# First loads and constant fills split and moved, masked keys in four steps on GpSimd, and a new order of all steps, in a two-layer transformer kernel

## The chip, the cores and the metric

One core of a Trainium2 chip. A time is the device time in microseconds of one execution; each version is given by the median of its runs. "The span" is the part of the profiled execution that the profiler's records cover. TensorE has two clock levels, 1.2 and 2.4 GHz; a granted clock of 0.5 in a row is the lower one, 1.0 the upper.

## The reference

Two layers are applied to x (16 sequences of 128 tokens, 128 features), each conditioned on a vector per sequence and on a context of 120 tokens. All in fp32. Cut to what matters:

```python
# layer 0 (c = cond, context = ctx), 16 heads of 8
shift_a, scale_a, gate_a, shift_m, scale_m, gate_m = split(silu(c) @ W_mod + b_mod, 6)
q, k, v = split(modulate(_ln(x), shift_a, scale_a) @ W_qkv + b_qkv, 3)
x = x + gate_a * (softmax(q k^T * scale) v @ W_proj + b_proj)
x = x + (cross attention of _ln(x) @ W_qc with _ln(context) @ W_kvc) @ W_cproj + b_cproj
x = x + gate_m * (gelu_tanh(modulate(_ln(x), shift_m, scale_m) @ W_mlp1 + b_mlp1) @ W_mlp2 + b_mlp2)
# layer 1: three adaptive norms (gamma, beta from c @ ln_w.T + ln_b), rope on q and k
x = x + attn(rope(q), rope(k), v) @ sa_out_w.T          # from adaln1(x) @ qkv_w.T
x = x + attn(rope(q), rope(k of context), v of context) @ ca_out_w.T
x = x + gelu_erf(adaln3(x) @ ffn_w1.T + ffn_b1) @ ffn_w2.T + ffn_b2
```

The modulation therefore consists of twelve vectors per sequence (six of layer 0, six of layer 1), each a product of a 128x128 weight block with the condition, plus a bias. The first self-attention needs only the first two of them, shift_a and scale_a.

## The kernel before

The 16 sequences are worked on in four **streams** of four sequences (CB = 4, so 512 tokens at a time). There are four attentions (a = 0: self, layer 0; 1: cross, layer 0; 2: self, layer 1; 3: cross, layer 1), so 16 **units** f = 4a + s, and eight MLPs m (four for each layer). x stays in SBUF throughout.

A unit goes through these steps. `stats` (VectorE, bn_stats and bn_aggr, L578 and L581) is followed by rstd on GpSimd (L744, L747); `ln` normalises (VectorE, xn, L588); `xT` transposes on TensorE (L873) and ScalarE applies the modulation while it copies (xnT, L829). `k`, `q`, `v` are the projections (L911, L918). In layer 1 rope follows on VectorE (L603, L608). `khi`/`qhi` round to the high part (ScalarE, Kh and Qh, L803 and L806), `klo`/`qlo` give the rest (VectorE, Kl and Ql, L617 and L620). `kstore`/`qstore` write these to DRAM, `kload`/`qload` read them back in the layout of the scores (Ks, Qd). `kmask` (GpSimd, Kd, L763) makes four copies of the keys, each with only the rows of some heads. `max` (TensorE L929, VectorE L683) finds the maximum of each row of scores, in four blocks b of four products each; `mT`, `mstore`, `mload` bring the maxima into a row of Qd. Then eight `score` steps (TensorE L949, exponential on ScalarE L843) and eight `value` steps (TensorE L966), `copy`, `norm`, `aT` and the output projection (`o` and `yT`, or `out`), which ends in an update of x (VectorE L727). An MLP has `stats`, `ln`, `xT`, four `h` (TensorE L992, GELU on ScalarE L860), and `h2` with `yT` (layer 0; L998) or `out` (layer 1; L1012).

The order of all this is written out by a table T of times (in steps, 16 to a unit), with one entry for each attention or layer: `make_plan` gives every step of every unit a time, sorts, and each engine issues its steps in that order, one after another. TensorE, GpSimd and the DMA queue of SyncE go by `plan`; VectorE and ScalarE go by `late`, the same list sorted by a second time, which differs only for `h`. An engine waits, by semaphores, where a step's input isn't there yet, and everything behind that step waits too. Five PSUM banks (ps_misc) are used in turn, in the order of `plan`.

Before the loop come the loads and the preparation. SyncE's queue issues x of stream 0, the 776 KB of modulation weights with the condition (`first`, which shares the tile hT), 512 KB of layer-0 weights, x of the other streams, the context twice, the other weights (1792 KB). ScalarE's queue issues the biases and the constants (identity, cos, sin). `small_in` counts three loads: `first`, biases, constants. GpSimd fills V (0, and 1 in the columns that sum), and, after the first rstd, Ks (1) and the two halves of Qd (0). VectorE makes `head_rows`, a sum over the identity, and inside the first `stats` the SiLU of the condition (`condition`, L627 to L631); TensorE then runs all twelve modulation products (L882), and VectorE adds the biases after the first `ln` (`modulation`, L639). ScalarE's first `xT` waits for all twelve.

## Time and profile before

| | us |
|---|---|
| median of 3 runs | 483.98 (481.41 to 486.79) |
| the profiled execution | 484.73 |
| its span | 482.9 |
| TensorE busy | 391.4 (81% of the span), mean granted clock 0.90 |
| VectorE busy | 330.1 (68%) |
| ScalarE busy | 267.9 (55%) |
| GpSimd busy | 159.0 (33%) |

An engine's busy share is a mean over the whole span: the stretches of the kernel have different limits, so the table is to be read with the rows by stretch below. Matmuls are pipelined and their ends are modelled, so TensorE's share says the least. An fp32 matmul shows up as two records.

### The profile page before, as it was taken

Reading aid. Unit: us, or ns where it says so; the run is one execution under the profiler, and the core shown is the slowest. Engines: PE = TensorE matmul, PEld = TensorE weight load, DVE = VectorE, ACT = ScalarE, POOL = GpSimd, SP = SyncE. Lnnn points to the kernel's source line nnn. Section 1 sums busy time; section 2 is a strip of 40 time slices with the busy share of each in tenths; the row PEclk is TensorE's granted clock in tenths of the full one; section 3 lists DMA queues with packets and bytes.
Section 4 is the critical chain, followed back from the end, with each engine's and each line's share of the span. In section 5 each row is a group of like instructions: output and inputs, shape, how many; then the busy total and the mean of one; then the engine's idle time right before and its main releaser. Section 6 shows DMA issues by size and latency. Waiting matters only on the chain.

```text
span 482.9 us, 9958 instructions
## 1 busy us (share of the span) xinstructions
PE 391.4 (81%) x3744; PEld 240.0 (50%) x3744; DVE 330.1 (68%) x841; ACT 267.9 (55%) x503; POOL 159.0 (33%) x138
## 2 busy tenths in 40 slices
PE   1555889888889797797987887989889898979686
PEld 1422455556555544434534534556565554737464
DVE  2656768999999837728648736799999884721331
ACT  1112457667676664565475554576576665666552
POOL 4764263455283401701601601335154161020130
PEclk9965599999999997978899958799999897979989
DMA  8860837558584516124225213346657551420001
GB/s 251 288 196 0 237 87 213 162 177 231 142 213 141 131 69 126 48 90 106 71 92 101 76 71 90 84 150 167 155 156 191 150 141 69 114 42 23 3 1 44
DMA packets 31271, 59.20 MB, mean 123 GB/s; under 512 B 3455, under 2 KB 7807, under 8 KB 30975
## 3 DMA queue, kind: packets, MB, share of 16 engines
q1 hardware_dynamic: 30935, 58.35, 43.9%
q8 instruction: 30, 0.49, 0.4%
q10 hardware_dynamic: 288, 0.21, 0.2%
q14 instruction: 18, 0.15, 0.1%
HBM read 31.81 MB, written 26.74 MB: 121 GB/s over the span
## 4 chain that ended last, share of the span: by engine, by line
PE 47%; DVE 21%; ACT 11%; POOL 9%; issue 5%; DMA 4%; SPq 2%; ACTq 0%; DVEq 0%; POOLq 0%
DVE maxima L683 8%; PE ps_misc L992 8%; PE ps_ao L966 8%; PE ps_misc L911 7%; POOL Kd L763 6%; PE ps_sc L949 6%; DVE xn L588 5%; PE ps_misc L1012 5%; ACT PT L843 5%; PE ps_misc L873 4%; ACT xnT L829 4%; PE ps_misc L998 3%; PE ps_misc L929 2%; POOL rstd L747 2%; DVE stats L578 2%
## 5 line engine op out<-in xcount | busy, mean ns | idle before, releaser
L843 ACT ACTIVATE PT<-ps_sc 128x512 f32<-128x512 f32 (+1 forms) x256 | 138.9, 596 | 79.8 <-PE ps_sc L949 79.0
L683 DVE TENSOR_REDUCE maxima<-ps_misc 128x4 f32<-128x512 f32 (+1 forms) x256 | 154.1, 666 | 29.4 <-PE ps_misc L929 29.1
L763 POOL TENSOR_SCALAR Kd<-Kh,head_rows 128x512 fp32r<-128x512 f32 (+1 forms) x64 | 98.6, 1556 | 114.2 <-ACT Kh L803 87.4
L949 PE MATMUL ps_sc<-Qd,Ks 57*128 57x256 f32 (+1 forms) x512 | 65.7, 335 | 18.6 <-ACT PT L843 15.6
L966 PE MATMUL ps_ao<-PT,V 120*18 120x128 f32 (+1 forms) x2048 | 71.6, 279 | 2.8 <-ACT PT L843 2.7
L744 POOL TENSOR_SCALAR vareps<-mv 128x4 f32<-128x4 f32 (+1 forms) x28 | 6.8, 242 | 188.5 <-DVE mv L581 188.0
L949 PEld LDWEIGHTS ps_sc<-Qd,Ks 57*128 57x128 f32 (+1 forms) x512 | 38.6, 187 | 55.7 <-ACT PT L843 28.4
L966 PEld LDWEIGHTS ps_ao<-PT,V 120*18 120x18 f32 (+1 forms) x2048 | 50.7, 99 | 20.9 <-issue 9.6
L829 ACT ACTIVATE xnT<-ps_misc,vec 128x128 f32<-128x128 f32 x80 | 30.1, 458 | 45.5 <-PE ps_misc L873 33.7
L911 PE MATMUL ps_misc<-xnT,W 128*128 128x512 f32 x72 | 47.5, 784 | 5.1 <-ACT xnT L829 5.1
L929 PE MATMUL ps_misc<-Kd,Qh 32*128 32x512 f32 (+1 forms) x256 | 45.3, 535 | 7.6 <-POOL Kd L763 6.5
L588 DVE TENSOR_SCALAR xn<-x,mv,rstd 128x128 f32<-128x128 f32 x96 | 36.6, 519 | 11.1 <-POOL rstd L747 11.1
L992 PE MATMUL ps_misc<-xnT,W 128*128 128x512 f32 x64 | 41.2, 803 | 3.7 <-ACT xnT L829 3.7
L727 DVE TENSOR_TENSOR x<-ps_misc,x 128x512 f32<-128x512 f32 x24 | 16.5, 688 | 38.1 <-PE ps_misc L1012 34.8
L873 PE MATMUL ps_misc<-cst,xn 128*128 128x128 f32 x96 | 18.5, 325 | 24.4 <-DVE xn L588 22.3
L929 PEld LDWEIGHTS ps_misc<-Kd,Qh 32*128 32x128 f32 x256 | 18.9, 197 | 26.2 <-issue 8.0
L860 ACT ACTIVATE hT<-ps_misc,bias 128x512 f32<-128x512 f32 x32 | 22.0, 687 | 16.7 <-PE ps_misc L992 16.4
L747 POOL TENSOR_TENSOR rstd<-vareps,minus_half 128x4 f32<-128x4 f32 (+1 forms) x28 | 29.3, 1047 | 2.3
L714 DVE TENSOR_SCALAR yT_sb<-ps_misc,bias,vec 128x128 f32<-128x128 f32 x32 | 10.9, 403 | 24.8 <-PE ps_misc L998 24.8
L992 PEld LDWEIGHTS ps_misc<-xnT,W 128*128 128x128 f32 x64 | 15.9, 262 | 23.8 <-issue 17.9
L873 PEld LDWEIGHTS ps_misc<-cst,xn 128*128 128x128 f32 x96 | 12.2, 163 | 29.8 <-issue 23.6
L911 PEld LDWEIGHTS ps_misc<-xnT,W 128*128 128x128 f32 x72 | 15.9, 246 | 19.6 <-issue 10.1
(75 smaller groups left out, 455.2 us busy)
## 6 DMA issues: line engine op xcount, KB each, us to landing
Qd<-q_mem SPq DMA_DIRECT2D x64, 192.0 KB
k_mem<-Kh SPq DMA_DIRECT2D x16, 512.0 KB, 3.2
q_mem<-Qh SPq DMA_DIRECT2D x16, 512.0 KB, 3.4
Ks<-k_mem SPq DMA_DIRECT2D x32, 192.0 KB
Ks<-k_mem SPq DMA_DIRECT2D x32, 180.0 KB
k_mem<-Kl SPq DMA_DIRECT2D x16, 256.0 KB, 3.6
q_mem<-Ql SPq DMA_DIRECT2D x16, 256.0 KB, 2.9
W<-weights SPq DMA_DIRECT2D x1, 1792.0 KB, 18.9
```

The lines of the kernel that those rows point to most:

```text
L588: dve.tensor_scalar(dst[0:rows, b, :], src[0:rows, b, :], mv[0:rows, which, b, 0:1], rstd[0:rows, which, b:b + 1], ALU.subtract, ALU.mult) ...
L683: dve.tensor_reduce(maxima[:, HG * n:HG * n + HG, st.b], bank(st.use + n)[:, 0:HG * ns].rearrange("p (h k) -> p h k", h=HG), AX_X, ALU.max ...
L747: pool.tensor_tensor(rstd[0:rows, which, :], vareps[0:rows, which, :], minus_half[0:rows, :], ALU.pow).then_inc(S["rstd_ready"], 1)
L763: pool.tensor_scalar(Kd[:, st.f % 2, c, 0:n], f32(Kh[:, st.f % 2, 0:n]), head_rows[:, c:c + 1], None, ALU.mult).then_inc(S["kd_ready"], 1)
L829: act.activation(dst[:, b * P:(b + 1) * P], src[:, b * P:(b + 1) * P], ACT.Identity, scale=vec[:, c, m:m + 1], bias=vec[:, c, sh:sh + 1]). ...
L843: act.activation(PT[0:ns, st.k % PSLOTS, g, :, :, :].rearrange("p i e t -> p (i e t)"), ps_sc[0:ns, g, :], ACT.Exp, scale=SCALE).then_inc( ...
L873: last = pe.transpose(bank(use)[:, b * rows:(b + 1) * rows], src[0:rows, b, :], ident[0:rows, 0:rows])
L911: pe.matmul(bank(st.use + i)[:, 0:n], w(f"{st.kind}{st.a}{form}"), src[:, 0:n], start=True, stop=True).then_inc(S["misc_filled"], 1)
L929: pe.matmul(bank(st.use + n)[:, 0:HG * ns], Qh[rows, st.f % 2, st.b * P:(st.b + 1) * P], Kd[rows, st.f % 2, :, st.b * ns:(st.b + 1) * ns], ...
L949: ins = pe.matmul(ps_sc[0:ns, side, i * E * P:(i + 1) * E * P], Ks[rows, st.f % 2, n, st.b * ns:(st.b + 1) * ns], Qd[rows, st.f % 2, n, :, ...
L966: last = pe.matmul(ps_ao[32 * c:32 * c + PAIR, st.b * P:(st.b + 1) * P], heads[:, at:at + PAIR], PT[0:ns, st.k % PSLOTS, c // E, odd, c % ...
L992: pe.matmul(bank(st.use), w(f"w1_{st.a}", st.j), xnT[:, feeds["mlp", st.m] % 2, :], start=True, stop=True).then_inc(S["misc_filled"], 1)
```

## The change

Four things are edited.

1. **Loads.** The condition (64 bytes a row) is loaded first, on its own, and only it counts for `small_in`. Then come x of stream 0, the first two of the twelve modulation blocks (128 KB, `mod_in0`), the layer-0 weights, x of stream 1, the other ten blocks (640 KB, `mod_in1`), and the rest as before.
2. **Modulation in two parts.** Two products stand ahead of the loop, with their two bias additions after the first `ln`. The other ten are a step of their own, `mods`, placed right behind the first `q` on TensorE and on VectorE. ScalarE's first `xT` waits for two vectors; the ones with another modulation wait for all.
3. **Fills.** VectorE fills the first half of Qd at the start; GpSimd fills Ks at the start, V only after the first `ln` (it waits for xn), and the second half of Qd behind the masked keys of unit 0. `head_rows` moves behind the first two bias additions, and VectorE's wait for the three small loads goes.
4. **Order.** `kmask` becomes four steps, spaced by kstep, so that others can fall between them, and many entries of T change.

```diff
@@ the table T (entries that change) @@
-    hstep=(0.0, 0.08),
+    hstep=(0.0, 0.01),
-    ln=(-36.9, -31.68, -33.31, -37.7),
-    xT=(-32.06, -29.2, -31.0, -33.04),
-    k=(-30.42, -33.11, -28.7, -30.27),
-    q=(-27.8, -25.66, -28.55, -28.51),
-    v=(-26.93, -32.58, -25.07, -25.11),
+    ln=(-36.9, -31.68, -33.31, -37.8),
+    xT=(-32.14, -29.39, -31.19, -33.23),
+    k=(-30.42, -32.7, -28.7, -30.22),
+    q=(-27.81, -25.66, -28.45, -28.51),
+    v=(-26.65, -32.58, -24.18, -25.26),
+    kstep=(0.3, 0.3, 0.3, 0.3),
-    max=(-23.26, -22.48, -23.15, -22.04),
-    mstep=(1.04, 0.96, 1.04, 0.85),
-    mT=(-9.62, -8.09, -7.7, -8.99),
+    max=(-23.26, -22.39, -23.06, -21.95),
+    mstep=(1.02, 1.02, 1.04, 0.85),
+    mT=(-9.62, -8.09, -8.17, -8.99),
-    copy=(1.29, -0.71, 0.74, 0.13),
-    norm=(2.85, 0.41, 2.69, 2.61),
+    copy=(1.29, -0.24, 0.74, 0.13),
+    norm=(2.69, 0.41, 2.69, 2.61),
...
-    yT=(10.12, 10.03, 6.38, 10.59),
+    yT=(9.35, 9.26, 5.61, 9.8),
-    mh=(9.79, 12.57),
-    mh2=(11.4, 15.76),
-    myT=(12.58, 13.02),
+    mh=(10.22, 13.1),
+    mh2=(11.43, 15.76),
+    myT=(11.93, 12.79),
...
-    qlo=(0.75, 1.08, 3.94, 3.39),
+    qlo=(0.75, 1.08, 5.75, 3.39),
-    value=(4.0, 3.57, 4.26, 5.04),
-    cln=(-39.87, -39.68, -41.82, -39.07),
+    value=(4.04, 3.61, 4.3, 5.07),
+    cln=(-40.26, -39.98, -42.12, -38.02),
...
@@ make_plan @@
-        at(t + T["kmask"][a], Step("kmask", **who))
+        for c in range(HG):
+            at(t + T["kmask"][a] + c * T["kstep"][a], Step("kmask", h=c, **who))
...
+    rest = Step("mods")
+    rest.late = [st for st in plan if st.kind == "q" and st.f == 0][0].late
+    plan.insert([st.kind for st in plan].index("q") + 1, rest)
@@ SyncE: loads @@
+                at, width = WCOLS["condT"]
+                sp.dma_start(first[:, at:at + width], weights[:, at:at + width]).then_inc(S["small_in"], 16)
                 load_x(0)
-                sp.dma_start(first, weights[:, 0:W_FIRST]).then_inc(S["small_in"], 16)
+                sp.dma_start(first[:, 0:MODS * D], weights[:, 0:MODS * D]).then_inc(S["mod_in0"], 16)
                 sp.dma_start(W[:, 0:W_SECOND - W_FIRST], weights[:, W_FIRST:W_SECOND]).then_inc(S["weights_in"], 16)
-                for s in range(1, STREAMS):
+                load_x(1)
+                sp.dma_start(first[:, MODS * D:at], weights[:, MODS * D:at]).then_inc(S["mod_in1"], 16)
+                for s in range(2, STREAMS):
                     load_x(s)
@@ VectorE @@
-                def modulation():
+                def modulation(part):
-                    dve.wait_ge(S["mod_products"], 1)
-                    for v in range(NV):
+                    dve.wait_ge(S["mod_products"], part + 1)
+                    for v in (range(MODS), range(MODS, NV))[part]:
...
                 dve.memset(ps_ao[:, :], 0.0).then_inc(S["sums_zeroed"], 1)
-                dve.wait_ge(S["small_in"], 48)
-                dve.tensor_reduce(head_rows[:, :], ident.rearrange("p (n c d) -> p c n d", n=NG, c=HG), AX_XY,
-                                  ALU.add).then_inc(S["rows_ready"], 1)
+                dve.memset(f32(Qd[:, 0, :, :, :]), 0.0).then_inc(S["zeros_ready"], 1)
...
                         if st.k == 0:
-                            modulation()
+                            modulation(0)
+                            dve.tensor_reduce(head_rows[:, :], ident.rearrange("p (n c d) -> p c n d", n=NG, c=HG),
+                                              AX_XY, ALU.add).then_inc(S["rows_ready"], 1)
+                    elif st.kind == "mods":
+                        modulation(1)
@@ GpSimd @@
                 fill(0, minus_half[:, :], -0.5)
-                fill(1, V[:, :, :, :, :], 0.0)
-                fill(2, V[:, :, :, :, HD:VW], 1.0)
+                fill(1, f32(Ks[:, :, :, :]), 1.0)
...
                         if st.norm_no == 0:
-                            fill(3, f32(Ks[:, :, :, :]), 1.0)
-                            for half in range(2):
-                                fill(4 + half, f32(Qd[:, half, :, :, :]), 0.0)
+                            pool.wait_ge(S["xn_ready"], CB)
+                            fill(2, V[:, :, :, :, :], 0.0)
+                            fill(3, V[:, :, :, :, HD:VW], 1.0)
                     elif st.kind == "kmask":
...
+                        if st.f == 0 and st.h == HG - 1:
+                            fill(4, f32(Qd[:, 1, :, :, :]), 0.0)
@@ ScalarE, xT @@
                         if st.k == 0:
+                            act.wait_ge(S["vec_ready"], MODS)
+                        elif st.spec["mult"] not in (None, MULT_A):
                             act.wait_ge(S["vec_ready"], NV)
@@ TensorE @@
+                def modulate(part):
+                    pe.wait_ge(S[f"mod_in{part}"], 16)
+                    for v in (range(MODS), range(MODS, NV))[part]:
+                        lhs, rhs = ((w_first("mod", v), silu[:, 2, :]) if v < 6 else
+                                    (w_first("ln", v - 6), condT))
+                        last = pe.matmul(ps_sc[:, part, v * B:(v + 1) * B], lhs, rhs, start=True, stop=True)
+                    last.then_inc(S["mod_products"], 1)
                 pe.wait_ge(S["silu_done"], 1)
-                for v in range(NV):
...
+                modulate(0)
...
+                    elif st.kind == "mods":
+                        modulate(1)
```

What the new times do to the order on each engine, unit by unit: the last block of `max` of unit 0 goes before `k` of unit 1 on TensorE, and the third block of `max` of unit 1 before `xT` of unit 2; in streams of the first attention a `score` step goes before the two `value` steps that stood ahead of it; in the MLPs of layer 0 the sixth `score` step goes before the four `h`, and `yT` before the seventh; in those of layer 1 two `value` steps or an `out` swap places with their neighbour; `qlo` of layer 1's self-attention moves behind the first block of `max`.

## Rows read from the trace of the kernel before

**Rows 1.** The page: busy us, share of the span and instructions of each engine.
```profile
PE 391.4 (81%) x3744; PEld 240.0 (50%) x3744; DVE 330.1 (68%) x841; ACT 267.9 (55%) x503; POOL 159.0 (33%) x138
```

**Rows 2.** Stretches: length, PE, PEld, DVE, ACT, POOL busy; clock, DMA share, GB/s.
```profile
117.00:136.00 19.00, 16.83 (x219) 11.18 (x215) 18.67 (x54) 13.19 (x26) 9.79 (x10) 1.00 0.64 173
...
180.00:320.00 140.00, 115.95 (x944) 65.27 (x944) 92.45 (x231) 75.44 (x139) 36.60 (x33) 0.84 0.33 87
```

**Rows 3.** Timeline, first 26 us: start us, busy us, engine, line, tiles, idle before.
```profile
8.41 0.86 DVE L578 BATCH_NORM_STATS2 stats<-x 128x6 f32<-128x128 f32 x4
...
10.09 1.05 POOL L747 TENSOR_TENSOR rstd<-vareps,minus_half 128x4 f32<-128x4 f32 x1
...
11.10 3.50 POOL L735 MEMSET Ks<- 128x4096 f32 x1
...
11.18 7.17 DVE L588 TENSOR_SCALAR xn<-x,mv,rstd 128x128 f32<-128x128 f32 x4 [0.94 <-POOL rstd L747]
...
14.66 7.13 POOL L735 MEMSET Qd<- 128x4096 f32 x2
...
18.27 1.79 DVE L639 TENSOR_SCALAR vec<-ps_sc,bias 128x16 f32<-128x16 f32 x12
...
18.40 1.11 PE L873 MATMUL ps_misc<-cst,xn 128*128 128x128 f32 x4 [2.81 <-DVE xn L588]
...
20.16 1.50 ACT L829 ACTIVATE xnT<-ps_misc,vec 128x128 f32<-128x128 f32 x4 [11.73 <-DVE vec L639]
...
21.71 3.52 PE L911 MATMUL ps_misc<-xnT,W 128*128 128x512 f32 x4 [2.19 <-ACT xnT L829]
```

**Rows 4.** Timeline, 0 to 37 us: fill of PSUM, modulation products, first masked keys, maxima.
```profile
0.91 0.48 DVE L643 MEMSET ps_ao<- 128x512 f32 x1 [0.91 <-PEq L1083]
...
12.88 2.72 PE L882 MATMUL ps_sc<-hT 128*128 128x16 f32 x12
...
24.61 6.20 POOL L763 TENSOR_SCALAR Kd<-Kh,head_rows 128x512 fp32r<-128x512 f32 x4 [2.81 <-ACT Kh L806]
...
31.69 4.88 DVE L683 TENSOR_REDUCE maxima<-ps_misc 128x4 f32<-128x512 f32 x8 [3.75 <-PE ps_misc L929]
...
36.48 1.11 DVE L588 TENSOR_SCALAR xn<-x,mv,rstd 128x128 f32<-128x128 f32 x4
```

**Rows 5.** DMA issues before 30 us: count, KB each, us from issue to landing.
```profile
x<-x_in SPq DMA_DIRECT2D x1, 256.0 KB, 4.6
...
cst<-consts ACTq DMA_DIRECT2D x1, 192.0 KB, 7.0
...
W<-weights SPq DMA_DIRECT2D x1, 512.0 KB, 7.7
...
W<-weights SPq DMA_DIRECT2D x1, 1792.0 KB, 18.9
```

**Rows 6.** Timeline of the ramp, 43 to 70 us.
```profile
43.25 1.89 DVE L683 TENSOR_REDUCE maxima<-ps_misc 128x4 f32<-128x512 f32 x3 [2.08 <-PE ps_misc L929]
...
61.28 0.69 ACT L806 ACTIVATE Kh<-ps_misc,bias 128x512 fp32r<-128x512 f32 x1 [1.28 <-PE ps_misc L911]
...
63.32 6.20 POOL L763 TENSOR_SCALAR Kd<-Kh,head_rows 128x512 fp32r<-128x512 f32 x4
```

**Rows 7.** Timeline of two MLPs of the first layer.
```profile
169.51 1.28 ACT L860 ACT_TABLE_LOAD   x1
...
169.59 3.67 PE L992 MATMUL ps_misc<-xnT,W 128*128 128x512 f32 x8 [0.62 <-ACT xnT L829]
...
170.80 1.47 ACT L860 ACTIVATE hT<-ps_misc,bias 128x512 f32<-128x512 f32 x2
...
174.13 3.67 PE L998 MATMUL ps_misc<-hT,W 128*128 128x512 f32 x8 [0.44 <-ACT hT L860]
...
206.44 6.72 PE L992 MATMUL ps_misc<-xnT,W 128*128 128x512 f32 x8 [0.48 <-ACT xnT L829]
```

**Rows 8.** One microsecond from the table of stretches, columns as in rows 2.
```profile
28.00:29.00 1.00, 0.00 (x0) 0.00 (x0) 0.00 (x0) 0.00 (x0) 1.00 (x1) 0.63 1.04 385
```

54 lines of the change are left out of this document (27 added, 27 removed).

## The prediction

> **What bounds the kernel now.** I read the page first for the shares. VectorE is busy for 68% of the span, TensorE for 81% [rows 1]: neither fills it, so the question is where each one is the limit, and the table of stretches answers it. From about 98 to 155 us VectorE is the limit: the stretch shown, a third of that, has it busy for 18.67 of 19 us [rows 2]. In such a stretch an order that only helps TensorE or ScalarE brings nothing. From 180 to 320 us no engine is full (VectorE 92 of 140 us, TensorE 116 at a mean granted clock of 0.84): a serial chain sets the time there, from the update of x over norm, transpose, keys, masked keys and the MLP to the next update [rows 2]. The timeline of the first 45 us shows that the whole pipeline starts late: the first key product runs at 21.71 us [rows 3] and the first maxima at 31.69 us [rows 4]. All queues run in order and wait for each other, not for a time of day. So what the first stage loses is lost at the end, and what it wins arrives there, unless something later eats it.
>
> **Why the start is late.** The four normalisations of the first stream (xn) should cost about 1.1 us, as the same four do for the second stream at 36.48 us [rows 4]. They take 7.17 us, from 11.18 to 18.35 [rows 3]. GpSimd fills Ks from 11.10 and the two halves of Qd from 14.66 on, at 3.5 us a fill, and VectorE gets through only once the second of these three fills has ended, at about 18.2 us. The Trainium skill (SBUF — State Buffer, § Who interferes with whom) says that VectorE's tensor_scalar in a two-port mode and GpSimd share a port pair that is held for a whole instruction, and the trace agrees (7.17 against 1.11 us). Then come twelve small bias additions, 1.79 us, all of which the first xnT waits for (20.16) [rows 3].
>
> **Part 1: loads and fills, up to the first key product.** After the change stream 0 waits for its own load alone. That load landed 4.6 us after its issue at 0.72, at 5.3 us [rows 5]; behind the small condT load it is issued some 0.45 us later, so 5.8. VectorE first fills Qd's first half: no VectorE fill of SBUF is in the trace; 512 elements of PSUM took 0.485 us [rows 4], so 4096 take 3.9, and I take 4, from 1.4 to 5.4 us. The low bound is half of that, the high one a wait for GpSimd's Ks fill (now from 0.9 to 4.4 us), which would end it at 8.4. So statistics 5.8 to 7.0, rstd at 8.3 (0.2 and 1.05 us and the hops between) [rows 3]. But the step `condition` stands before xn in VectorE's queue and waits for the constants, which landed 7.0 us after 1.16, at 8.2 [rows 5]; the bytes in flight around them are hardly fewer, so I keep 8.2 (bound: 7.3, where rstd decides). The exponential and the three small steps end at 9.1. xn is then 9.1 to 10.2, since GpSimd now waits for xn before it fills V. Only two of twelve products stand before the transposes, 0.9 us by the rate of [rows 4] (12 records, six products, in 2.72 us: some 0.44 us a product), and two additions, 0.3 us. The transposes took 1.1 us and the xnT 1.5 us [rows 3]: 10.3 to 11.4, 11.5 to 13.0. **First key product at 13.1 instead of 21.7 us: 8.6 us gained.** Its weights landed 7.7 us after 1.62, at 9.3 [rows 5], with more ahead of them than now.
>
> The Trainium skill (SBUF — State Buffer, § Who interferes with whom) says that a VectorE instruction outside the two-port modes with at most one SBUF input does not contend with GpSimd, and VectorE: DVE Perf Modes (§ Zero memsets can be issued as uint32) that a memset takes a cycle per element; no run here shows either yet. By these the fill ends near 5.7 us and the sum stays; were the port shared after all, the sum would be 2.4 us worse, 479.4.
>
> **Part 2: what the other ten products cost.** They now stand behind the first q. On TensorE that is 10 x 0.44 = 4.4 us, from 3.5 us after the key product to 7.9, and v (1.0 us) follows: 9.0. The masked keys are done 2.9 + 6.2 = 9.1 us after the key product, as before (24.61 and 6.20 against 21.71) [rows 4], so TensorE's part is hidden under GpSimd's. VectorE's is not quite: it sits in order behind these products until 7.9, then adds ten biases (1.5), computes Ql (0.75) and the statistics of stream 1 (1.25): free for the first maxima at 11.55, where it was at 9.98 (31.69 - 21.71). **1.6 us lost.** Ql's store comes later with it, at about 23.5 us, but its reader, the first score, is some 25 us away. The load of these ten weights is issued fifth; about 1.8 MB lie before its end, and the load of 512 KB had landed at 9.3 with as much asked for. Lower bound for its landing 9, upper bound 24.2, where the last large load landed [rows 5]; needed at 16.6.
>
> **Part 3: fills behind the first masked keys.** V's fill, smaller than those of 3.5 us, takes GpSimd from 10.2 to at most 13.7, under a wait for Kh until 16. The fill of Qd's second half, 3.5 us, now stands before the rstd of stream 1, which would be ready 14 us after the key product; its reader, xn of stream 1, comes after eight maxima (5.3 us), at 16.9. Hidden; without that cover it would cost up to 3.5.
>
> **Part 4: masked keys as four steps.** Sorting both tables of times, only one of GpSimd's neighbours changes: the statistics of stream 0's context (cstats) fall between the second and third quarter of the masked keys of unit 3. It brings one rstd forward by two quarters (3.1 us) and delays two quarters by 1.3 us, in the stretch where VectorE is the limit. I take zero. In the serial stretch the norm before each MLP still stands behind all four quarters (6.2 us), so the split doesn't shorten that chain.
>
> **Part 5: order in the ramp, 38 to 70 us.** The last maxima products of unit 0 now go before the next key product. VectorE had waited 2.08 us for them [rows 6]. Most of that is cut off by unit 1's masked keys, which start no earlier for it. Statistics of stream 3 come earlier, so GpSimd no longer makes unit 2's masked keys wait for their rstd: they started at 63.32 though Kh had been there since 61.97 [rows 6]. **I take this 1.3 us as gained** (0 to 2.1).
>
> **Part 6: order in the serial stretch.** In the four MLPs of the first layer one pair of exponentials (1.08 us) moves from behind the four GELUs to before them, between xnT and the table load of 1.28 us [rows 7]. TensorE's first product isn't ready before the load ends, so load and exponentials no longer fit under it: for the first MLP, exponentials to 170.6, load to 171.9, four GELUs of 0.7 to 174.7. The second product, which waits for all four and began at 174.13, starts at 174.85, 0.7 us later, and with it the update of x. Where the clock is low the GELUs are paced by TensorE (6.72 instead of 3.67 us for the first product) [rows 7] and nothing is lost. Two MLPs are of each kind: **1.4 us lost** (0 to 2.8). The Trainium skill (ScalarE: Activation LUTs, § What ACT_TABLE_LOAD costs) adds a drain of 1.38 us to each switch; here hT starts 0.01 us after the load's end, so the trace speaks against it and I give it no chance; by the page the sum would be 2.8 us worse, 479.8. Elsewhere scores now go before a pair of values in streams 0 to 3, but mostly where VectorE is the limit: zero. In the second layer and at the tail such swaps change at most 1 us in either direction: zero.
>
> **The sum.** -8.6 + 1.6 - 1.3 + 1.4 = -6.9 us. The profiled execution took 484.73 us (span 482.9), so 477.8; the median of the three runs is 483.98, 0.75 below, so I forecast 477.0. Its own range is 472 to 481 (bounds of parts 1, 5 and 6, and the clock). About 1% is what a measurement of this kernel can tell from no change.
>
> **Rivals.** (A) *The lead is gone before the first maxima.* The ten products hold VectorE's queue: if TensorE's clock is low there, as it is from the 29th microsecond on now [rows 8], they take 8.8 instead of 4.4 us, and the time is 481.4; if their weights land only with the last large load, at 24.2, the first maxima come at 32 and nothing is left of the lead: 484. For it: the clock falls in a microsecond in which TensorE had nothing to do [rows 8]. Against: the DMA order puts these weights fifth, and TensorE has work at 10, 11 and 13 us. (B) *Given back later.* The GELU delay hits all four MLPs, with a missed slot in the chain (masked keys before rstd, 6.2 us) once: -8.6 + 1.6 + 2.8 + 1.3 gives 481. For it: that chain has no slack. Against: GpSimd's order there is unchanged. (C) *The clock turns against it: slower.* Of the eight MLPs, four run their first products at the low clock, as the one at 206.44, and four at the high one, as the one at 169.59 [rows 7]. Place: the products behind xnT, where the moved pair of scores and values shifts TensorE's work. Price 3.05 us each [rows 7]. From three of four on, the 7 us are gone; with all four it is 489.2, slower by 1.1%. Against: the relative order around them is nearly the same. (D) *More than summed*: the clock turns the other way for two or more (6.1 us, 470.9), or xn is held back less by masked keys. (E) *The start isn't shortened*, because xn is stretched anyway: 484. Against: no fill is left that could run beside it, so I fold it into (A).
>
> **How the numbers follow.** Forecast as summed 0.60, (A) with (E) 0.19, (B) 0.10, (C) 0.05, (D) 0.06. Faster by over 1% (below 479.1): forecast and (D), 0.66. Within 1%: (A) and (B), 0.29. Slower: (C), 0.05. The range reaches down into (D) and up over most of (A) and (B): 472 to 482.5; about 0.05 lies below and 0.12 above.
>
> **What would show it.** xn of stream 0 at 1.1 us; the first key product at 12.3 to 13.5 us; the ten later products ending about 8 us after it and the first maxima 11.5 us after it; the first score 7 to 9 us earlier; VectorE's full stretch of the same length; first GELU 1.1 us later after xnT in the MLPs at the high clock; the number of MLPs with slow first products still four. I'd be wrong if the constants land later than 8.2 us, if the ten weights land after 17, or if the distance from the first score to the end grows by over 3 us.

## The result: 2% slower, not 1.4% faster

| | before | after |
|---|---|---|
| median, us | 483.09 (481.41 to 486.79, 4 runs) | 493.62 (492.53 to 496.31, 4 runs) |
| ratio after / before | | 1.0192, 95% interval 1.0144 to 1.0240 |
| profiled execution, us (span) | 484.73 (482.9) | 492.53 (490.7) |
| first key product, us | 21.71 | 12.75 |
| first maxima on VectorE, us | 31.69 | 22.44 |

Ratios, here and below, leave out single executions that ran slower than the others of their kernel, so a ratio can differ from the quotient of the two medians.

The forecast was 477.0 us with a range of 472 to 482.5. The kernel lies 11 us above that range. The head start is there, and in this execution larger than forecast (9.25 us at the first maxima, forecast 7.0); the rest of the kernel takes some 17 us more.

The page of the profile after, busy us, share and instructions of each engine (as [rows 1]):

```profile
PE 396.4 (81%) x3744; PEld 244.2 (50%) x3744; DVE 327.1 (67%) x842; ACT 266.2 (54%) x503; POOL 155.1 (32%) x137
```

The work is nearly the same. TensorE's busy time grew by 5.0 us at the same number of instructions (mean granted clock 0.89 after, 0.90 before); that of the other three engines fell by 2 to 4 us. So for VectorE, ScalarE and GpSimd the 8 us more of span are idle time. Where? First the timeline of the first 26 us after (start us, busy us, engine, line, operation, tiles, number; in brackets the engine's idle time before it and who ended it), which answers to [rows 3, 4]:

```profile
0.88 3.51 POOL L748 MEMSET Ks<- 128x4096 f32 x1
...
2.23 3.47 DVE L655 MEMSET Qd<- 128x4096 f32 x1 [0.84 <-issue]
...
6.26 0.21 ACT L794 ACTIVATE silu<-hT 128x16 f32<-128x16 f32 x1 [3.34 <-DMA cst<-consts]
...
8.87 1.12 DVE L599 TENSOR_SCALAR xn<-x,mv,rstd 128x128 f32<-128x128 f32 x4 [0.94 <-POOL rstd L759]
...
11.20 1.50 ACT L845 ACTIVATE xnT<-ps_misc,vec 128x128 f32<-128x128 f32 x4 [4.72 <-PE ps_misc L889]
...
12.75 3.50 PE L932 MATMUL ps_misc<-xnT,W 128*128 128x512 f32 x4 [1.59 <-ACT xnT L845]
...
15.65 6.20 POOL L775 TENSOR_SCALAR Kd<-Kh,head_rows 128x512 fp32r<-128x512 f32 x4 [2.12 <-ACT Kh L820]
...
16.90 1.49 PE L900 MATMUL ps_sc<-hT 128*128 128x16 f32 x12
...
18.43 1.52 DVE L650 TENSOR_SCALAR vec<-ps_sc,bias 128x16 f32<-128x16 f32 x10 [2.09 <-PE ps_sc L900]
...
22.44 3.68 DVE L696 TENSOR_REDUCE maxima<-ps_misc 128x4 f32<-128x512 f32 x6 [0.65 <-PE ps_misc L952]
```

xn is 1.12 us and no longer 7.17, the key product starts 8.96 us earlier and the first maxima 9.25 us earlier. Up to here nothing went wrong.

A marker follows the lead further: ScalarE copies the turned maxima (maxT) exactly once in each of the 16 units (a unit is one attention of one stream; attention 0 has units 0 to 3, attention 1 has 4 to 7). Its start, before and after, in us:

| unit | 0 | 1 | 2 | 3 | 4 | 5 | 6 | 7 | 9 | 11 | 13 | 15 |
|---|---|---|---|---|---|---|---|---|---|---|---|---|
| before | 46.91 | 66.84 | 86.98 | 106.61 | 126.01 | 145.85 | 166.64 | 200.94 | 275.84 | 336.35 | 374.48 | 421.46 |
| after | 34.87 | 58.98 | 80.03 | 101.70 | 126.49 | 150.13 | 172.89 | 211.54 | 288.33 | 344.80 | 384.51 | 428.70 |
| after - before | -12.0 | -7.9 | -7.0 | -4.9 | +0.5 | +4.3 | +6.3 | +10.6 | +12.5 | +8.5 | +10.0 | +7.2 |

The lead of 12 us (7.9 with the new start alone, e16) is down to 7 at unit 2, is gone by unit 4, and 6 us more are lost by unit 6. The 13 us between units 2 and 6 are lost where VectorE had been full: before, from about 98 to 155 us, of which [rows 2] shows a part. The table of stretches after, 80 to 160 us (length, then PE, PEld, DVE, ACT, POOL busy; granted clock, DMA share, GB/s):

```profile
80.00:100.00 20.00, 17.49 (x213) 11.59 (x214) 17.00 (x51) 12.52 (x25) 9.26 (x9) 0.91 0.60 162
100.00:120.00 20.00, 15.02 (x166) 9.79 (x164) 15.08 (x40) 10.52 (x21) 5.00 (x5) 0.87 0.71 202
120.00:140.00 20.00, 17.62 (x209) 10.92 (x207) 17.32 (x52) 11.88 (x23) 7.85 (x9) 0.93 0.51 136
140.00:160.00 20.00, 18.35 (x207) 11.79 (x203) 16.46 (x50) 10.60 (x20) 7.77 (x8) 0.86 0.41 121
```

VectorE is no longer full there: it is busy 65.9 of 80 us. Before, it was busy 76.7 us of the same stretch. And TensorE's granted clock, 1.00 in each of these four rows before, is now 0.86 to 0.93. The engine that set the pace waits; the next rows show for what. Timeline after, around the worst place (unit 5's keys and values):

```profile
109.52 1.12 PE L939 MATMUL ps_misc<-W,cnT 128*120 128x128 f32 x8
...
111.06 1.11 DVE L599 TENSOR_SCALAR xn<-x,mv,rstd 128x128 f32<-128x128 f32 x4
...
113.39 0.50 PE L974 MATMUL ps_sc<-Qd,Ks 57*128 57x256 f32 x4 [2.75 <-DMA Qd<-m_mem]
...
113.83 1.07 PE L991 MATMUL ps_ao<-PT,V 128*18 128x128 f32 x32
115.02 0.61 ACT L830 ACTIVATE V<-ps_misc 120x512 f32<-120x512 f32 x1 [5.16 <-PE ps_ao L991]
115.52 0.65 ACT L820 ACTIVATE Kh<-ps_misc,bias 128x480 fp32r<-128x480 f32 x1
...
116.20 0.72 DVE L631 SCALAR_TENSOR_TENSOR Kl<-ps_misc,bias,Kh 128x480 fp32r<-128x480 f32 x1 [4.04 <-ACT Kh L820]
116.27 2.96 POOL L775 TENSOR_SCALAR Kd<-Kh,head_rows 128x480 fp32r<-128x480 f32 x2 [5.91 <-ACT Kh L820]
```

Read it from the bottom. GpSimd stands 5.91 us and VectorE 4.04 us for Kh. Kh stands behind ScalarE's copy of V, which waited 5.16 us. V has three buffers (VSLOTS = 3), so unit 5's copy waits for the last value product of unit 2, at 113.83. That product now stands behind the first score of unit 3 (113.39), which waited 2.75 us for its load of the maxima. Three order changes meet in this chain: Kh behind V (ScalarE), values behind the next score (TensorE), and a late load (SyncE). SyncE's own queue, after, shows why the load is late:

```profile
101.98 0.50 SPq L556 DMA_DIRECT2D m_mem<-maxT  x1
102.52 1.15 SPq L523 DMA_DIRECT2D k_mem<-Kh  x1
```

Unit 4's Kh has been there since 91.8 us, but its store stands behind the store of unit 3's maxima, which waits for those maxima (engine and line, who is waited for: us in total, times, longest):

```profile
SPq L556 <- ACT maxT L852: 10.6, 1, 10.6
```

So the stores and then the loads of Qd, which follow in the same queue, all go out in one bunch from 102 to 109 us.

### The profile page after: what moved, and what is told of

The parts are those of the page before. It is cut to its first block, busy times and chain, and to the rows that moved or that the text cites. A ratio compares the mean times of both kernels' runs of the same rounds, so it can differ in the third digit from the quotient of the medians.

```text
span 490.7 us, 9979 instructions
## 1 busy us (share of the span) xinstructions
PE 396.4 (81%) x3744; PEld 244.2 (50%) x3744; DVE 327.1 (67%) x842; ACT 266.2 (54%) x503; POOL 155.1 (32%) x137
## 4 chain that ended last, share of the span: by engine, by line
PE 50%; ACT 18%; DVE 13%; issue 6%; POOL 6%; DMA 4%; SPq 3%; ACTq 0%; DVEq 0%; POOLq 0%
PE ps_sc L974 8%; PE ps_ao L991 8%; PE ps_misc L932 8%; ACT PT L859 7%; PE ps_misc L1037 5%; POOL Kd L775 5%; DVE maxima L696 5%; PE ps_misc L952 5%; PE ps_misc L889 4%; PE ps_misc L1023 3%; ACT hT L876 3%; PE ps_misc L1017 3%; PE ps_misc L1000 3%; ACT xnT L845 3%; PE ps_misc L939 2%
## 5 line engine op out<-in xcount | busy, mean ns | idle before, releaser
L974 PE MATMUL ps_sc<-Qd,Ks 57*128 57x256 f32 (+1 forms) x512 | 68.9, 349 | 25.3 <-ACT PT L859 20.4
L991 PE MATMUL ps_ao<-PT,V 120*18 120x128 f32 (+1 forms) x2048 | 75.9, 290 | 3.4 <-ACT PT L859 3.4
L952 PE MATMUL ps_misc<-Kd,Qh 32*128 32x512 f32 (+1 forms) x256 | 50.1, 542 | 13.7 <-POOL Kd L775 6.7
L932 PE MATMUL ps_misc<-xnT,W 128*128 128x512 f32 x72 | 46.5, 770 | 2.7 <-ACT xnT L845 2.5
L952 PEld LDWEIGHTS ps_misc<-Kd,Qh 32*128 32x128 f32 x256 | 21.1, 200 | 35.6 <-issue 9.6
L599 DVE TENSOR_SCALAR xn<-x,mv,rstd 128x128 f32<-128x128 f32 x96 | 28.7, 361 | 10.1 <-POOL rstd L759 10.1
L1017 PE MATMUL ps_misc<-xnT,W 128*128 128x512 f32 x64 | 31.8, 643 | 3.5 <-ACT xnT L845 3.5
L704 DVE RECIPROCAL rden<-ps_misc 128x32 f32<-128x32 f32 x32 | 11.3, 354 | 26.8 <-PE ps_misc L1000 26.6
L1000 PE MATMUL ps_misc<-cst,AOs 128*128 128x128 f32 x128 | 23.6, 314 | 6.1 <-ACT AOs L865 5.0
L727 DVE TENSOR_SCALAR yT_sb<-ps_misc,bias,vec 128x128 f32<-128x128 f32 x32 | 10.9, 404 | 22.8 <-PE ps_misc L1023 22.0
L830 ACT ACTIVATE V<-ps_misc 128x512 f32<-128x512 f32 (+1 forms) x16 | 9.8, 612 | 28.3 <-PE ps_misc L939 16.6
L932 PEld LDWEIGHTS ps_misc<-xnT,W 128*128 128x128 f32 x72 | 15.7, 245 | 16.8 <-issue 10.5
```

The costliest lines, as they stand in the source:

```text
L932: pe.matmul(bank(st.use + i)[:, 0:n], w(f"{st.kind}{st.a}{form}"), src[:, 0:n], start=True, stop=True).then_inc(S["misc_filled"], 1)
L952: pe.matmul(bank(st.use + n)[:, 0:HG * ns], Qh[rows, st.f % 2, st.b * P:(st.b + 1) * P], Kd[rows, st.f % 2, :, st.b * ns:(st.b + 1) * ns], ...
L974: ins = pe.matmul(ps_sc[0:ns, side, i * E * P:(i + 1) * E * P], Ks[rows, st.f % 2, n, st.b * ns:(st.b + 1) * ns], Qd[rows, st.f % 2, n, :, ...
L991: last = pe.matmul(ps_ao[32 * c:32 * c + PAIR, st.b * P:(st.b + 1) * P], heads[:, at:at + PAIR], PT[0:ns, st.k % PSLOTS, c // E, odd, c % ...
L1000: last = pe.transpose(bank(st.use)[:, b * P:(b + 1) * P], AOs[:, st.k % 2, b * P:(b + 1) * P], ident)
L1017: pe.matmul(bank(st.use), w(f"w1_{st.a}", st.j), xnT[:, feeds["mlp", st.m] % 2, :], start=True, stop=True).then_inc(S["misc_filled"], 1)
```

## The experiments

In all of them the numbers to watch are the time and the marker of unit 6 (start of its maxT copy). Five of the kernels below have the same order up to there, but for one pair of small steps in kmask_split (start_only, start_again, kmask_split, late_new, mlp_alone), and their markers lie at 158.0 to 160.0 us; so one trace gives it to about 1 us either way, better than a time does.

A part of that scatter is made at the start. In e16 the ten later modulation products take 4.3 us, where in the kernel after they took 2.3 (16.09 to 18.39):

```profile
16.22 1.73 PE L900 MATMUL ps_sc<-silu,hT 128*128 128x16 f32 x8
17.79 2.72 PE L900 MATMUL ps_sc<-hT 128*128 128x16 f32 x12
```

So it is in e1, e3, e8, e11, e14 and e15 too, and in these seven the first maxima come at 23.8 to 24.0 us. In the other nine traces with the early start they take 2.3 to 2.8 us, and the first maxima come at 22.3 to 22.8. The granted clock from 16 to 18 us is 1.00 in all sixteen; what decides between them stays open. Within either kind the markers compare best: e14 with e16, e6 with e12.

**The two halves apart: e1_start_only, e2_order_only.** e1 is the changed kernel with the table of times of before, e2 the reverse (start of before, new table, four kmask steps). On the chip of these two and the next two the kernel before took 485.76 us.

```diff
@@ e1: after.py, table T @@
-    ... all new entries, kstep=(0.3, 0.3, 0.3, 0.3)
+    ... the entries of before, kstep=(0.0, 0.0, 0.0, 0.0)
@@ e2: before.py, table T and kmask @@
+    ... all new entries, kmask as four steps
```

> The new loads, fills and split modulation, with the old table of times (masked keys still issued four in a row). If the new start does what its rows say (first maxima 9.3 us earlier than before) and nothing there is given back, this runs at 483.1 - 9 = 474 us, 472 to 476. If the early start itself breaks something later (transfers of keys and maxima colliding with the last large load, a shifted clock), it comes out above 480.

> The old start with the new table of times and the four masked-key steps. If the order is what costs, all of it is here: 493.6 + 9 = 502 us, 499 to 505. If the loss comes from start and order together, it stays under 495.

e1: 476.41 us, ratio 0.9813 (0.9768 to 0.9857); unit 6 at 159.1. e2: 503.34 us, ratio 1.0382 (1.0337 to 1.0428); unit 6 at 183.1. The start alone brings 9 us here (7.4 in its repeat, e16), and it is kept to the end. The order alone costs 18 us, and within the intervals it costs the same on the late start as on the early one (1.0192 / 0.9813 = 1.039). So the change is the sum of a good part and a bad one.

**Two suspects put back in the changed kernel: e3_k_back, e4_value_back.**

```diff
@@ e3 @@
-    k=(-30.42, -32.7, -28.7, -30.22),
+    k=(-30.42, -33.11, -28.7, -30.22),
@@ e4 @@
-    value=(4.04, 3.61, 4.3, 5.07),
+    value=(4.0, 3.57, 4.26, 5.04),
```

> The changed kernel with one number put back: k of the second attention at -33.11, so that ScalarE rounds Kh before it copies V, as before. Theory 'Kh behind V' (V waits for the values of three units earlier, and Kh, masked keys and Kl stand behind it in ScalarE's, GpSimd's and VectorE's queues): most of the loss between unit 3 and unit 7 (15.5 us) goes, 480 us, 477 to 485. Theory 'score before values' (TensorE waits for maxima with values behind it): 491 to 494.

> The changed kernel with the old times of value (4.0, 3.57, 4.26, 5.04), so that a pair of values goes before the score step again in streams 0 to 3. Theory 'score before values': the waits of TensorE for a unit's maxima no longer hold the previous unit's last values, V comes free earlier, 480 to 484 us. Theory 'Kh behind V' alone: Kh still waits for V, but V waits less; a gain of 3 to 6 us, 488 to 491.

e3: 488.2 us, ratio 0.9981 (0.9936 to 1.0026). e4: 486.75 us, ratio 0.9969 (0.9918 to 1.0019), unit 6 at 167.6 (172.9 in the changed kernel). Each of the two wins back about 2 of the 4% that the order costs, so neither is the whole cause. (The profiled execution of e3 is 4 us above its median, so its marker isn't used.) Both kernels scatter over 16 us in ten runs, where the kernel before scattered over 4 in nineteen.

**Both back, and each alone on the early start: e5 to e8.** On another chip, kernel before at 484.67 us.

```diff
@@ e5: after.py with both of the above @@
@@ e6: e1 with @@
-    k=(-30.42, -33.11, -28.7, -30.27),
+    k=(-30.42, -32.7, -28.7, -30.27),
@@ e7: e1 with @@
-    value=(4.0, 3.57, 4.26, 5.04),
+    value=(4.04, 3.61, 4.3, 5.07),
@@ e8: e1 with the new entries of attentions 2 and 3 and of the MLPs @@
```

> The changed kernel with two steps of its new order put back for attention 1 and the scores: the key projection of attention 1 at -33.11 (ahead of the value copies of its queue) and the value products of attention 0 at their old times (ahead of the next unit's score). Theory that these two steps carry the loss of units 0 to 7: the time is that of the early start with the old order (476.4), 475 to 479, ScalarE's maxima copies of units 0 and 7 lie 154 to 158 us apart (176.7 in the changed kernel). Rival, other steps of the new order (the update of x before the maxima on VectorE, the mask stores on SyncE) cost as much: 482 to 487 and 163 us or more.

> The early start with the old order (476.4), and only the key projection of attention 1 moved from -33.11 to -32.7. TensorE's and GpSimd's orders are unchanged; on ScalarE the copy of V comes before the copy of Kh, on VectorE a normalisation before Kl, on SyncE a mask store before a key store, in the four units of attention 1. Theory that this step alone costs about half of the loss: 481 to 485, units 0 to 7 about 161 to 165 us apart in ScalarE's maxima copies (155.9 without it). Rival, it costs only together with the other changes of the order: 475 to 478, 155 to 158 us.

> The early start with the old order (476.4), and only the value products at their new times: TensorE's queue has a unit's score ahead of the last value pair of the stream before it, in the streams of attention 0. Theory that this step alone costs the other half: 481 to 485, units 0 to 7 161 to 165 us apart. Rival, it costs only where the score comes late for another reason: 475 to 478, 155 to 158 us.

> The early start, the old order in attentions 0 and 1, the new one from attention 2 on. Theory that the loss is made in units 0 to 7 alone: units 0 to 7 as in the early start with the old order (154 to 158 us), and the whole 474 to 478. Rival, the new order of the second half costs too and was hidden by what the first half had lost: 479 or more.

| | ratio (interval) | median | unit 6 |
|---|---|---|---|
| e5_both_back | 1.0024 (0.9979 to 1.0068) | 486.24 | 162.4 |
| e6_k_alone | 0.9985 (0.9938 to 1.0033) | 485.40 | 169.1 |
| e7_value_alone | 0.9936 (0.9897 to 0.9974) | 480.24 | 161.2 |
| e8_late_new | (4 runs, 471.98 to 482.35) | 478.16 | 158.7 |

One number, k from -33.11 to -32.7, takes away the whole gain of the start: e6 is back at the time of before. The value products alone cost only about 2 us at the marker (4 to 6 by the ratios), yet in the changed kernel putting them back wins 5.3: they cost more where a score is late for another reason. e5 refutes "these two are all" by its time, which is no better than with either of them alone put back, though its marker (162.4 against 172.9) says that they carry 10.5 of the 13.3 us lost up to unit 6. So something costs behind unit 6. e8 has the new order only there and lies between its two expectations; with runs from 472 to 482 it settles nothing by itself.

**The rest of the early order, one swap each: e9 to e12.** On a third chip, kernel before at 485.46 us.

```diff
@@ e9: e1 with @@
-    mstore=(-3.29, 0.82, 1.19, -2.35),
+    mstore=(-3.65, 0.82, 1.19, -2.35),
@@ e10: e1 with @@
-    yT=(10.12, 10.03, 6.38, 10.59),
+    yT=(9.35, 9.26, 6.38, 10.59),
@@ e11: e5 with mstore[0], yT[0] and yT[1] of before too @@
@@ e12: e1 with (SyncE's order kept) @@
-    k=(-30.42, -33.11, ...)   kstore=(2.28, 2.86, ...)
+    k=(-30.42, -32.7, ...)    kstore=(2.28, 2.45, ...)
```

> The early start with the old order (476.4; 155.9 us between ScalarE's maxima copies of units 0 and 7), and one thing moved: on SyncE the store of unit 3's maxima stands ahead of the key store of unit 4. Theory that this swap is part of the loss: it holds back the key store of unit 4 and the loads behind it, 1 to 3 us once, 157 to 159 us and 477 to 479. Rival, the loss of the key projection's move is all on ScalarE and VectorE: 155 to 157 us, 475 to 477.5.

> The early start with the old order, and only the updates of x of attentions 0 and 1 at their new times: VectorE updates x of units 1, 2 and 3 before the first maxima of a later unit, not behind them, and TensorE turns y before the score that it stood behind. Theory that this is most of what is left of the loss when key projection and value products are back (164.4 us between the maxima copies of units 0 and 7): 161 to 165 us, 480 to 484. Rival, it costs under 2 us and the rest lies in the ramp: 155 to 158 us.

> The changed kernel with four steps put back: the key projection of attention 1, the value products of attention 0, the mask store of attention 0, and the updates of x of attentions 0 and 1. Theory that these four carry the loss: 155 to 158 us between the maxima copies of units 0 and 7 (176.7 in the changed kernel, 155.9 with the old order), 472 to 478. Rival, the new order of the ramp costs (TensorE's projections and maxima swapped in units 0 to 2): 159 or more, 479 or more.

> The early start with the old order, and the key projection of attention 1 moved to -32.7 with its store kept at the old time: SyncE's order is the old one, and only ScalarE's copy of V before that of Kh, and VectorE's normalisation before Kl, are left of the move. Theory that ScalarE's copy of Kh behind V is what costs: about as e6, 163 to 166 us between the maxima copies of units 0 and 7 and 481 to 486. Rival, the mask store ahead of the key store on SyncE was most of it: 156 to 159 us, 475 to 479.

| | ratio (interval) | median | unit 6 |
|---|---|---|---|
| e9_mstore_alone | 0.9891 (0.9823 to 0.9958) | 478.11 | 159.2 |
| e10_update_alone | 0.9851 (0.9775 to 0.9927) | 477.81 | 158.0 |
| e11_four_back | 0.9942 (0.9909 to 0.9976) | 482.22 | 159.8 |
| e12_k_no_swap | 0.9965 (0.9932 to 0.9998) | 482.61 | 164.6 |

SyncE's swap costs nothing clear of the scatter alone (159.2; the five lie at 158.0 to 160.0), but together with the late Kh it costs 4.4 us at the marker (e6 at 169.1 against e12 at 164.6; the intervals of the two ratios overlap): a miss of its first theory, and again a cost that needs company. The updates of x are free, a clear miss (expected 480 to 484). With four steps back, unit 6 is at 159.8, so the ramp's new order is worth nothing there either way. The last two of the four, SyncE's swap and the updates of x, are worth 2.6 us there together (e5 at 162.4). But e11's time is still 5 to 6 us above the start alone (e1, e16): that part is lost behind unit 6.

**The last three questions: e13 to e16.** On the second chip again, kernel before now at 483.77 us; e16 is e1 once more, as the measure.

```diff
@@ e13: e1 with the new hstep, mh, mh2, myT @@
-    hstep=(0.0, 0.08),   mh=(9.79, 12.57),
+    hstep=(0.0, 0.01),   mh=(10.22, 13.1),
@@ e14: e1 with (VectorE's and SyncE's orders kept) @@
-    k=(-30.42, -33.11, ...)   klo=(1.98, 1.19, ...)
+    k=(-30.42, -32.7, ...)    klo=(1.98, 0.78, ...)
@@ e15: e1 with @@
-    kstep=(0.0, 0.0, 0.0, 0.0),
+    kstep=(0.3, 0.3, 0.3, 0.3),
```

> The early start with the old order, and only the MLPs' times new: in the four MLPs of layer 0, TensorE's and ScalarE's score pair 5 of the stream beside it stands ahead of the four hidden products and their GELUs. Theory that this step is what the new order costs behind unit 6 (kernels with the new order there took 2.7 us more after unit 6 than those with the old one, by their medians less the time of unit 6's maxima copy): 1.5 to 4 us above the early start alone. Rival, as predicted at 0.7 us in each MLP at the full clock, of which the trace has two: 1.4. Rival, nothing: within 1 us of the early start alone.

> The early start with the old order, and one kind of swap on one engine: in units 4 to 7 ScalarE copies V ahead of Kh. VectorE's, TensorE's, GpSimd's and SyncE's orders are the old ones. Theory that this swap alone carries what is left of the key projection's move without SyncE's swap: ScalarE's maxima copy of unit 6 at 163 to 166 us (159.1 with the old order, 164.6 with VectorE's swap in it too), 480 to 484. Rival, VectorE's normalisation ahead of Kl was the cost: 158 to 160 us and 475 to 479.

> The early start with the old order, and the four masked key slots as steps 0.3 apart instead of one after the other. Theory of the prediction (nothing: the steps' order on GpSimd stays, but for one pair of small operations ahead of the last slot of unit 3): within 1 us of the early start alone, unit 6 at 158 to 160 us. Rival, the statistics of the context that now stand between slots delay the slot that the maxima wait for: unit 6 at 161 or more.

> The early start with the old order a second time, as the measure for the three beside it on the same chip: 475 to 479, ratio to the kernel before 0.977 to 0.99, unit 6 at 157 to 160 us.

| | ratio (interval) | median | unit 6 |
|---|---|---|---|
| e13_mlp_alone | 0.9894 (0.9849 to 0.9939) | 478.46 | 158.0 |
| e14_kh_behind_v | 1.0043 (1.0013 to 1.0073) | 485.36 | 168.9 |
| e15_kmask_split | 0.9831 (0.9790 to 0.9871) | 475.54 | 159.0 |
| e16_start_again | 0.9853 (0.9818 to 0.9887) | 476.42 | 160.0 |

e14 differs from e16 in nothing but this: in four units ScalarE copies V before Kh and not after. It costs 8.9 us, more than the start brings there (7.4). The mean granted clock of the two profiled executions is the same (0.915 and 0.917), so the clock is not the reason. The same place (unit 4) in the two traces, e16 first:

```profile
87.38 0.66 ACT L820 ACTIVATE Kh<-ps_misc,bias 128x480 fp32r<-128x480 f32 x1
88.14 5.92 POOL L775 TENSOR_SCALAR Kd<-Kh,head_rows 128x480 fp32r<-128x480 f32 x4 [0.35 <-ACT Kh L820]
...
88.90 0.72 DVE L631 SCALAR_TENSOR_TENSOR Kl<-ps_misc,bias,Kh 128x480 fp32r<-128x480 f32 x1 [0.19 <-DMA k_mem<-Kl]
89.26 0.62 ACT L830 ACTIVATE V<-ps_misc 120x512 f32<-120x512 f32 x1 [1.22 <-PE ps_ao L991]
```

And e14:

```profile
89.68 0.61 ACT L830 ACTIVATE V<-ps_misc 120x512 f32<-120x512 f32 x1 [1.92 <-PE ps_ao L991]
90.19 0.65 ACT L820 ACTIVATE Kh<-ps_misc,bias 128x480 fp32r<-128x480 f32 x1
90.87 0.72 DVE L631 SCALAR_TENSOR_TENSOR Kl<-ps_misc,bias,Kh 128x480 fp32r<-128x480 f32 x1 [1.74 <-ACT Kh L820]
90.94 6.00 POOL L775 TENSOR_SCALAR Kd<-Kh,head_rows 128x480 fp32r<-128x480 f32 x4 [2.73 <-ACT Kh L820]
```

V waits for an old unit's values either way. In e16 Kh has already passed, and ScalarE waits for V with nobody behind it. In e14 Kh is behind that wait: it comes 2.8 us later, with it GpSimd's four masked slots, and VectorE, the engine that sets the pace, stands for Kl. VectorE's waits from 80 to 160 us (engine, line, who is waited for: us in total, times, longest), first e16's only one on Kl, then e14's:

```profile
DVE Kl L631 <- DMA k_mem<-Kl: 0.2, 1, 0.2
```

```profile
DVE Kl L631 <- ACT Kh L820: 8.0, 4, 2.2
```

Four units, 2.0 us each, 8.0 us: that is nearly all of the 8.9 us of the time and of the marker's 8.8 (160.0 to 168.9). That is shown. It also says why e12 is milder (164.6): there VectorE does a normalisation first, which is ready, and half of the stall is filled:

```profile
DVE Kl L631 <- ACT Kh L820: 4.0, 4, 1.3
```

The changed kernel has that normalisation in front too, so for ScalarE's swap e12 is the nearer measure; with its values and stores late as well, VectorE's waits for Kh in the same stretch come to 6.4 us in it.

e15 measures the split of the masked keys at -0.9 us of 476.4: nothing. (There the statistics that come between the quarters fall one quarter later than in the changed kernel.) e13 measures the MLPs' new order at +2.0 us, with intervals that overlap. One MLP of layer 0, e16 first:

```profile
162.88 1.28 ACT L876 ACT_TABLE_LOAD   x1
162.97 3.67 PE L1017 MATMUL ps_misc<-xnT,W 128*128 128x512 f32 x8 [0.62 <-ACT xnT L845]
...
167.38 1.28 ACT L859 ACT_TABLE_LOAD   x1
167.48 0.30 PEld L1023 LDWEIGHTS ps_misc<-hT,W 128*128 128x128 f32 x2 [0.63 <-issue]
167.51 3.67 PE L1023 MATMUL ps_misc<-hT,W 128*128 128x512 f32 x8 [0.44 <-ACT hT L876]
```

and e13:

```profile
160.86 1.08 ACT L859 ACTIVATE PT<-ps_sc 120x512 f32<-120x512 f32 x2
...
160.96 3.67 PE L1017 MATMUL ps_misc<-xnT,W 128*128 128x512 f32 x8 [0.20 <-ACT xnT L845]
...
161.96 1.28 ACT L876 ACT_TABLE_LOAD   x1
...
163.25 2.42 ACT L876 ACTIVATE hT<-ps_misc,bias 128x512 f32<-128x512 f32 x4
...
165.82 3.67 PE L1023 MATMUL ps_misc<-hT,W 128*128 128x512 f32 x8 [1.18 <-ACT hT L876]
...
172.18 1.28 ACT L859 ACT_TABLE_LOAD   x1 [6.50 <-PE ps_sc L974]
173.47 1.09 ACT L859 ACTIVATE PT<-ps_sc 120x512 f32<-120x512 f32 x2
```

From the first product to the second it is 4.54 us in e16 and 4.86 in e13: 0.3 us from the exponentials that now stand ahead. From the second product to the end of the update of x it is 6.58 us in all four MLPs of both. The other item is the last load, which delays the scores' side. In e16 ScalarE reloads the table of exponentials at 167.38, at once after the GELUs and beside TensorE's second product. In e13 it first waits 6.50 us for the next score and then loads, so 1.28 us stand bare between score and exponentials. The groups of these six loads (busy, mean ns | idle time before them, and who ended it), e16 and then e13:

```profile
L859 ACT ACT_TABLE_LOAD x6 | 7.7, 1283 | 2.0 <-PE ps_sc L974 2.0
```

```profile
L859 ACT ACT_TABLE_LOAD x6 | 7.7, 1283 | 26.2 <-PE ps_sc L974 26.2
```

In e13 ScalarE stands 26.2 us in front of loads, four times 6.5, once for each MLP of layer 0. It had idle time there before too (2.94 us in e16, ahead of the exponentials at 172.70), and no run separates what the bare load costs.

**Behind unit 6, over all kernels.** A kernel's median less its marker of unit 6 is what the rest takes. The ten kernels with the old order there (before, e1, e6, e7, e9, e10, e12, e14, e15, e16) give 316.4 to 319.8 us, on average 317.5; five with the new one (after, e2, e4, e5, e11) give 319.2 to 323.9, on average 321.3. (e3 is left out, and e8, whose executions fall into two pairs 6 us apart.) Median and marker come from different executions, up to 4 us apart; with the profiled execution's own time the averages are 316.7 and 320.1. So the new order costs some 3.3 to 3.8 us behind unit 6. The MLPs' part of it is 1.2 (e13 against e16, profiled time less marker) to 2.0 us (medians), not clear of the scatter; the rest I have not located.

## Why the prediction was wrong

**The start (parts 1 to 3) was right, and a little better than said.** Predicted: key product at 13.1, measured 12.75. The constants had landed by 6.3 us and not at 8.2, so that rstd decided, which was the low bound. VectorE's fill took 3.47 us beside GpSimd's 3.51, where I had taken 4 us; that it ended at 5.70, near my 5.4, is in part luck, as it also began 0.8 us later than taken. It wasn't held up to 8.4. By the Trainium skill (SBUF — State Buffer, § Who interferes with whom) such a fill doesn't contend with GpSimd, and the trace agrees (2.23 to 5.70 beside 0.88 to 4.39). Part 2 took ten products at 0.44 us each, and VectorE free 11.55 us after the key product (its printed terms, 7.9, 1.5, 0.75 and 1.25, add to 11.4). In the changed kernel's trace the products ran at 0.23 (16.09 to 18.39 for all ten) and the first maxima came 9.7 us after the key product, so the +1.6 became -0.3; in e16 they ran at 0.43, the first maxima came 11.2 us after it, and the term is +1.2, nearly as said. The lead at the first maxima is thus 9.25 us in the one and 7.9 in the other. V's fill and that of Qd's second half were hidden: rstd of stream 1, behind the fill, ended at 26.75 and its xn began at 27.23, among the maxima. e1 and e16 put the whole at -7.4 to -9.4 us against -7.0: right.

**Rivals (A) and (E)** are refuted by the same rows. The ten weights' load was there in time, the ten products took 2.3 to 4.3 us and never 8.8, and xn was not stretched (1.12 us). **Rival (B)** had the delay in all four MLPs right (e13 waits 6.50 us before each of the four loads), but its 481 us is far below the 493.6 measured, and it had nothing before the MLPs.

**Part 4, the split, zero: right** (e15: -0.9, within the scatter).

**Part 5, the ramp, -1.3: right in kind, wrong in result.** VectorE's wait before unit 0's last maxima went, and unit 0's marker came forward (36.3 in e11 against 39.0 in e16). By unit 1 it was gone (59.2 against 59.5), as the step held, and by unit 6 too (159.8 against 160.0). The 1.3 us that I did count are there where I placed them: unit 2's masked keys start 0.1 us after Kh's end in e11 and 1.35 us in e16. But Kh itself comes 0.8 us later (54.60 against 53.84), so they start only 0.5 us earlier, and the marker of unit 2 shows nothing of it (79.7 against 78.9).

**Part 6, the MLPs, +1.4: the size may be right, the working isn't.** 0.3 and not 0.7 us come from the delayed GELUs in an MLP at the high clock, because they then run back to back (2.42 us for four) and no longer at TensorE's pace. What I didn't see is the second table load of 1.28 us, pushed behind a wait, in all four MLPs. Together e13 puts the MLPs at 1.2 to 2.0 us, not clear of the scatter; all that lies behind unit 6 is 3.3 to 3.8. The Trainium skill (ScalarE: Activation LUTs, § What ACT_TABLE_LOAD costs) adds a drain of 1.38 us at each switch, which part 6 weighed. In e13 hT starts 0.01 us after the load's end, so the trace still speaks against it.

**The step that failed** is the sentence "Elsewhere scores now go before a pair of values in streams 0 to 3, but mostly where VectorE is the limit: zero", and with it what opened the prediction: in a stretch where VectorE is the limit, "an order that only helps TensorE or ScalarE brings nothing". No run here speaks against that, but I read it as "an order there costs nothing". It has two sides. A full engine can't gain from its neighbours' order, but it can lose by it, since it stays full only while each of its inputs is ready in its turn. Of the neighbours' swaps there I weighed TensorE's and one of GpSimd's. The swap that costs most alone, Kh behind V on ScalarE in units 4 to 7, isn't mentioned in the prediction at all, nor in the list of swaps ahead of it; it came from one number, k of attention 1, later by 0.41 in the table, which on TensorE changes no order. ScalarE's half of that step sits 0.4 behind it, and so slid past v by 0.28.

The account, at unit 6 and then at the end, in us against before:

| | predicted | shown |
|---|---|---|
| start | -7.0 | -7.1 at unit 6 (mean of e1 and e16; -6.6 to -8.6 over the five), -7.4 to -9.4 at the end |
| Kh behind V on ScalarE (units 4 to 7) | not named | +8.9 alone (e14); +5 with VectorE's normalisation first (e12) |
| ... with SyncE's late key store | not named | +4.4 more (e6 over e12); nothing clear without the late Kh (e9) |
| values behind the next score | 0 | about +2 alone (e7), +5.3 in company (e4 against after) |
| updates of x, split of masked keys, ramp | -1.3 | about 0 alone; updates with SyncE's swap +2.6 in company (e5 over e11) |
| behind unit 6 | +1.4 | +3.3 to +3.8 |
| sum | -6.9 | -7.1 + 13.3 + 3.8 = +10.0, measured +10.5 |

The 13.3 us are what the order costs up to unit 6 in the changed kernel (172.9 against 159.55, the mean of e1 and e16). They are not the sum of the rows between, whose costs depend on each other. By putting things back they are reached step by step: 5.3 for the values (e4), 10.5 for values and k together (e5), 13.1 for all four (e11).

**Rival (C)**, the one on the slow side, had the right sign and the wrong cause. I'd said the number of MLPs with slow first products would stay four, and more of them would make it slower. It did not stay four: over all eight MLPs, four were slow before (6.72, 6.71, 6.30 and 6.63 us) and one is after (6.10, in layer 1); all four of layer 0 take 3.67. By the group of all 64 of these products it is 41.2 us before and, after:

```profile
L1017 PE MATMUL ps_misc<-xnT,W 128*128 128x512 f32 x64 | 31.8, 643 | 3.5 <-ACT xnT L845 3.5
```

TensorE needs 9.4 us less for them, and the kernel is slower all the same. Its clock over the whole stretch is no higher for it: over 180 to 320 us it was 0.84 before [rows 2] and is 0.84 after. (D) counted 3.05 us for each MLP whose products turn fast; here three more are fast than before, and nothing of the 9 us shows in the time.

**What I had said would refute me** did: "if the distance from the first score to the end grows by over 3 us". It grew by 18.6 us: the first score started at 55.59 before and at 44.80 after, in spans of 482.9 and 490.7. And "VectorE's full stretch of the same length" was the right thing to look at: 65.9 of 80 us after, against 75.5 in e16.

The best version here is the start alone: 476.4 us on two chips, 1.5 to 1.9% faster than before; with the masked keys split (e15, 475.5) or with the updates of x at their new times (e10) it is the same.

## What to carry to other kernels

When all steps get new times, sort the table once for every engine, not only for the ones that look busy, and for each pair that swaps ask what the instruction in front waits for. A copy that waits for a buffer to come free is harmless as the last in a row and can cost its whole wait, on every engine that reads what is behind it, as soon as something needed is queued after it. In the stretch where an engine is full, no neighbour's swap brought a gain here, but some cost; and such waits chain, so that a swap that costs nothing clear alone (SyncE's) can cost 4 us beside another. Measure the parts apart before judging the sum: here a gain of 1.7% and a loss of 3.8% came as one change.
